# Graph norm of a GNN kernel: variance with features on partitions instead of along the row

## What is computed

```
def _batchnorm(x, g, b):
    mu = jnp.mean(x, axis=0)
    var = jnp.mean((x - mu) ** 2, axis=0)
    return (x - mu) * jax.lax.rsqrt(var + EPS) * g + b
...
return _batchnorm(conv_out + h_attn + h, norm2_g, norm2_b)
...
x = x + _L1_gnn_ref(_layernorm(x, axis=-1), ...)
x = x + _L1_ffn_ref(_layernorm(x, axis=-1)[None], ...)[0]
```

## Time and profile before

| | us |
|---|---|
| median of 3 runs | 1284.91 (1284.19 to 1285.83) |
| profiled execution, own time | 1289.82 |
| its span | 1288.10 |
| granted TensorE clock, mean of the span | 0.983 of full speed |
| TensorE busy | 1219.5 (95%) |
| VectorE busy | 547.9 (43%) |
| ScalarE busy | 452.7 (35%) |
| GpSimd busy | 227.7 (18%) |

### The profile page before, as it was taken

The page is one execution under the profiler, slowest core; times in us unless marked ns, Lnnn a source line. Parts: engine busy times, 40 slices in busy tenths (PEclk is TensorE's granted clock), DMA queues, the critical chain, the costliest instruction groups (busy, mean ns, idle before and its releaser), DMA issues. The chain is left out here.

```text
span 1288.1 us, 19378 instructions
## 1 busy us (share of the span) xinstructions
PE 1219.5 (95%) x6528; PEld 814.0 (63%) x6529; DVE 547.9 (43%) x1535; ACT 452.7 (35%) x965; POOL 227.7 (18%) x227
## 2 busy tenths in 40 slices
PE   4999899999999899999999999999989999989898
PEld 2555476468448555478877887786555587564465
DVE  8999743433443344110000000001296345675784
ACT  6878533233223310011111111111123343338873
POOL 1000070030000008311111111111273000025540
PEclk9999899999999989999999999999998999999899
DMA  9300000000003300671165312564562010100011
GB/s 221 91 1 1 1 2 1 0 2 2 0 6 126 130 2 1 203 273 42 44 245 182 115 44 70 216 236 148 167 186 98 1 35 1 74 0 1 1 31 52
DMA packets 42978, 98.25 MB, mean 76 GB/s; under 512 B 4142, under 2 KB 6632, under 8 KB 41874
## 3 DMA queue, kind: packets, MB, share of 16 engines
q1 hardware_dynamic: 28642, 68.70, 16.0%
q0 software_dynamic: 6144, 16.45, 4.6%
q10 hardware_dynamic: 8112, 12.08, 2.6%
HBM read 81.02 MB, written 16.17 MB: 75 GB/s over the span
## 5 line engine op out<-in xcount | busy, mean ns | idle before, releaser
L498 PEld LDWEIGHTS psum<-sb_blk,sb_w_reg 128*128 128x128 f32 x1792 | 204.0, 192 | 12.8 <-issue 12.8
L498 PE MATMUL psum<-sb_blk,sb_w_reg 128*128 128x128 f32 x1792 | 205.2, 275 | 1.7 <-issue 1.7
L2145 PE MATMUL psum<-sb_z_reg_r,sb_hT_conv_r 125*125 125x512 f32 x385 | 156.9, 408 | 0.4 <-DVE sb_z_last L1262 0.4
L1434 DVE TENSOR_TENSOR sb_blk<-sb_blk,psum 128x256 f32<-128x256 f32 x56 | 23.6, 421 | 277.0 <-ACT sb_blk L955 277.0
L2145 PE MATMUL psum<-sb_htok_r,sb_hT_conv_r 125*125 125x512 f32 x285 | 112.9, 396 | 0.0
L498 PE MATMUL psum<-sb_hT_conv,sb_w_reg 128*128 128x416 f32 (+3 forms) x336 | 103.6, 465 | 0.8 <-ACT sb_hT_conv L532 0.8
L2235 PE MATMUL psum<-sb_w_reg,sb_blk 128*128 128x512 f32 x224 | 100.8, 592 | 0.0
L498 PEld LDWEIGHTS psum<-sb_hT_conv,sb_w_reg 128*128 128x128 f32 x336 | 63.8, 193 | 35.9 <-issue 33.0
L2145 PEld LDWEIGHTS psum<-sb_z_reg_r,sb_hT_conv_r 125*125 125x125 f32 x385 | 72.0, 187 | 18.0 <-issue 0.7
L2067 PE MATMUL psum<-sb_w_reg,sb_hT_conv 128*125 128x512 f32 x160 | 83.1, 613 | 0.0
L955 ACT ACTIVATE sb_blk<-psum 128x256 f32<-128x256 f32 x56 | 21.5, 384 | 162.9 <-PE psum L498 160.1
(11 more groups left out here) (452 smaller groups left out, 2002.3 us busy)
## 6 DMA issues: line engine op xcount, KB each, us to landing
sb_hT_conv<-w_expert SPq DMA_DIRECT2D x7, 2048.0 KB, 9.8
sb_w_reg<-w_expert SPq DMA_DIRECT2D x6, 2048.0 KB, 18.1
sb_hT_conv<-w_expert SPq DMA_DIRECT2D x7, 1024.0 KB, 12.4
slot_outs<-sb_blk ACTq DMA_DIRECT2D x28, 256.0 KB
sb_w_reg<-w_expert SPq DMA_DIRECT2D x6, 1024.0 KB, 19.9
sb_w_reg<-w_gnn SPq DMA_DIRECT2D x1, 4096.0 KB
sb_w_reg<-w_qkv SPq DMA_DIRECT2D x1, 3072.0 KB, 21.5
slot_outs<-sb_blk ACTq DMA_DIRECT2D x1, 2560.0 KB, 13.1
```

The costliest lines, as they stand in the source:

```text
L498: ins = e.matmul(out, l, r, start=(n == 0), stop=(n == len(pairs) - 1))
L1434: e.tensor_tensor(hidT[:, 2 * h:2 * h + 2, :].rearrange("p k n -> p (k n)"), silg[:, h, :], psum[:, 1 + h, HF:2 * HF], ALU.mult).then_inc( ...
L2145: ins = e.matmul(psum[0:TP, b, :], counts_at(l, 2 * i + n // NT)[:, s % HALF_T, :], z[s], start=(n == 0), stop=(n == len(pairs) - 1))
```

## The change

The squares become the stationary operand, in four blocks of 128 features, and the first column of `mean_w` the moving one, so that the variance stands as 128 partitions x 4 columns in bank 1. These columns are set to zero first by a matmul with a zeroed operand, since four accumulations share the bank. The root and the reciprocal are taken of 128x4. VectorE multiplies the identity by each of the four columns, and TensorE multiplies a matrix of ones by the four results, which puts the row of 512 reciprocals into 125 rows of bank 1; VectorE multiplies that by the norm's weights into `sc2`. The four ones matmuls stand behind the first two values products on TensorE, the other six behind them, and three filler matmuls remain of eight. The semaphore `centered` is now called `stat_vec` and counts the four products too.

```diff
--- before.py
+++ after.py
@@ -348,9 +348,12 @@
         rden = s3[:, 228:244].rearrange("p (t h) -> p t h", t=2)
         bst = s3[:, 250:322].rearrange("p (k c s) -> p k c s", k=KD, c=3)
         bmv = s3[:, 322:330].rearrange("p (k s) -> p k s", k=KD)
+        none4 = s3[0:TP, 340:340 + KD]
         bsc, bsh = s3[:, 330:334], s3[:, 334:338]
         squares = a_reg[0:TP, 0:NT * D].rearrange("p (t n) -> p t n", n=D)
         sc2 = w_reg[0:TP, 1, 1552:1552 + D]
+        by_feature = a_reg[:, 0:D].rearrange("p (k c) -> p k c", k=KD)
+        std4 = a_reg[:, D:D + KD]
         scale = DH ** -0.25
         inv_root_m = M_FEAT ** -0.5
 
@@ -468,8 +471,8 @@
         at_turned, attnT_in, ha_mm, ha_in, shifted = (
             sem(n) for n in ("at_turned", "attnT_in", "ha_mm", "ha_in", "shifted"))
 
-        conv_added, y_ready, stat_mm, centered, squared, searched, var_std, scaled_vec, scaled_pool, x_two = (
-            sem(n) for n in ("conv_added", "y_ready", "means_and_variances", "centered", "squared", "rest_searched",
+        conv_added, y_ready, stat_mm, stat_vec, squared, searched, var_std, scaled_vec, scaled_pool, x_two = (
+            sem(n) for n in ("conv_added", "y_ready", "means_and_variances", "stat_vec", "squared", "rest_searched",
                              "var_std", "scaled_vec", "scaled_pool", "x_two"))
 
         ia_mm, ia_in, chosen_pool, proc_mm, acts_in = (
@@ -1180,10 +1183,10 @@
 
             e.wait_ge(neigh_mm, 4 * NT)
             for i in range(NT):
-                e.wait_ge(centered, i + 1)
+                e.wait_ge(stat_vec, i + 1)
                 e.square(squares[:, i, :], htok[:, i, :]).then_inc(squared, 1)
             e.wait_ge(stat_mm, 2)
-            e.activation(sc2, psum[0:TP, 1, :], ACT.Sqrt, bias=eps[0:TP, :]).then_inc(var_std, 1)
+            e.activation(std4, psum[:, 1, 0:KD], ACT.Sqrt, bias=eps).then_inc(var_std, 1)
             for j in range(4):
                 e.wait_ge(pv_mm, j + 1)
                 e.copy(w_po_flat[:, j * 512:(j + 1) * 512], psum[:, 4 + j, :]).then_inc(pv_in, 1)
@@ -1974,6 +1977,7 @@
             for n, i in enumerate(Y_ORDER):
 
                 if n == 2:
+                    e.memset(none4, 0.0).then_inc(v_own, v.up())
                     e.wait_ge(y_ready, 2)
                     e.tensor_tensor(y_sum, htok[:, Y_ORDER[0], :], htok[:, Y_ORDER[1], :], ALU.add).then_inc(v_own, v.up())
                 elif n > 2:
@@ -1989,11 +1993,14 @@
                                 ALU.add).then_inc(y_ready, 1)
             e.wait_ge(stat_mm, 1)
             for i in range(NT):
-                e.tensor_tensor(htok[:, i, :], htok[:, i, :], psum[0:TP, 0, :], ALU.subtract).then_inc(centered, 1)
+                e.tensor_tensor(htok[:, i, :], htok[:, i, :], psum[0:TP, 0, :], ALU.subtract).then_inc(stat_vec, 1)
             e.wait_ge(var_std, 1)
-            e.reciprocal(sc2, sc2).then_inc(v_own, v.up())
-            e.wait_ge(v_own, v.n)
-            e.tensor_tensor(sc2, sc2, rows3[:, 1, :], ALU.mult).then_inc(scaled_vec, 1)
+            e.reciprocal(std4, std4).then_inc(v_own, v.up())
+            e.wait_ge(v_own, v.n)
+            for k in range(KD):
+                e.tensor_scalar(by_feature[:, k, :], ident, std4[:, k:k + 1], None, ALU.mult).then_inc(stat_vec, 1)
+            e.wait_ge(stat_mm, 3)
+            e.tensor_tensor(sc2, psum[0:TP, 1, :], rows3[:, 1, :], ALU.mult).then_inc(scaled_vec, 1)
             e.wait_ge(scaled_vec, 1)
             e.wait_ge(squared, NT)
             for t in range(NT + 3):
@@ -2598,16 +2605,26 @@
                 pe_conv_sum(e, flag, i)
             e.wait_ge(y_ready, NT)
             e.matmul(psum[0:TP, 0, :], mean_w, y_sum, start=True, stop=False)
+            e.matmul(psum[:, 1, 0:KD], ident[0:TP, :], none4, start=True, stop=False)
             e.wait_ge(y_ready, NT + 1)
             e.matmul(psum[0:TP, 0, :], mean_w, htok[:, NT - 1, :], start=False, stop=True).then_inc(stat_mm, 1)
             for i in range(NT):
                 e.wait_ge(squared, i + 1)
-                ins = e.matmul(psum[0:TP, 1, :], mean_w, squares[:, i, :], start=(i == 0), stop=(i == NT - 1))
+                for k in range(KD):
+                    ins = e.matmul(psum[:, 1, k:k + 1], squares[:, i, k * 128:(k + 1) * 128], mean_w[:, 0:1],
+                                   start=False, stop=(i == NT - 1 and k == KD - 1))
             ins.then_inc(stat_mm, 1)
             e.wait_ge(ha_in, 4)
-            for k in range(8):
+            for k in range(2):
                 pe_values(e, k)
-            pe_busy(e, 2, w_o[:, 0, :], 8)
+            for k in range(KD):
+                e.wait_ge(stat_vec, NT + k + 1)
+                ins = e.matmul(psum[0:TP, 1, k * 128:(k + 1) * 128], one16[:, 0:1].to_broadcast([128, TP]),
+                               by_feature[:, k, :], start=True, stop=True)
+            ins.then_inc(stat_mm, 1)
+            for k in range(2, 8):
+                pe_values(e, k)
+            pe_busy(e, 2, w_o[:, 0, :], 3)
 
             for i in range(NT):
                 e.wait_ge(ln_out, 3 * NT + i + 1)
```

## The result

The changed kernel is slower. The first comparison gave a median of 1297.63 us (1292.68 to 1298.51, 4 executions) against 1285.37 (1284.19 to 1286.01, 4): ratio 1.0087, interval 1.0066 to 1.0108, so 8.5 to 13.9 us. It was compared twice more, beside the experiments: 1.0055 (1.0042 to 1.0068) and 1.0049 (1.0034 to 1.0064), so 4.4 to 8.8 us. The forecast was +7.4 us with 1288.4 to 1295.2; the direction came true, the first median lies 2.4 us above the range.

A forecast was written before the change was run, and what follows sets the result against it. Bound: TensorE's squares, a 4.9 us serial chain, then VectorE's tile loop. Squares +6.9, serial part +0.0, ScalarE's queue +1.4, GpSimd -0.95 gave +7.4: 1292.3 us, range 1288.4 to 1295.2.

The forecast's parts named there:

- Squares, +6.9 forecast: TensorE's squares as 80 one-column records, 0.214 us each at 1.2 GHz, end at 1128.9 against 1122.0 us: +6.9.
- I take 1.2 GHz for the whole stretch: Squares: the clock has already fallen when they begin and one-column work does not raise it; 17.1 us for 80 loads.
- a sign against it: Changed profile, squares: a granted clock of 1.00 during them would show the forecast wrong.
- lower bound: Range's low side: a fall 2.6 to 3.5 us after short work begins ends squares up to 3.4 us earlier, 1288.9.
- Serial part, +0.0 forecast: Root to scales: 4.9 us again, the reciprocal's gain taken by half-speed values products and the ones matmuls.
- ScalarE's queue against GpSimd, +1.4 - 0.95 forecast: Before the first turn: VectorE waits 1.4 us for ScalarE's copies and root; GpSimd's earlier end gives back 0.95.
- Filler, 0 forecast, at most +1.5: Ahead of the turns: five removed fillers hide entirely; TensorE idles 2.3 us, up to +1.5 if the clock falls.
- The clock coming back on continuously issued loads: Rival at the squares: weight loads keep TensorE busy, full clock from 1114.7; 1284.2 us, same; chance 0.12.
- The rival of a full clock throughout: Rival at the squares: no fall ahead of them and the clock holds, 8.6 us of loads; 1282.4 us; chance 0.02.
- The half case: Squares: full clock for part of the stretch, 3 to 4 us less, about 1288.6 us; chance 0.10.
- first rival: Squares: the clock comes back all the same at 1114.7; 1284.2 us, no change that can be told; chance 0.12.
- I carry the difference over to the median: Whole kernel: the profiled execution, 4.91 us above the median, gives the change in time, +7.4, added to 1284.9.

The follow-up runs named there:

- wide: Changed kernel with all 125 columns of mean_w moving in the squares' matmuls in place of one; 1285.35 us against 1287.28 for the kernel before, ratio 0.9986.
- after_again: The changed kernel as it is, compared and traced once more; 1293.02 us against 1287.28 for the kernel before, ratio 1.0055.
- late_copies: Changed kernel with ScalarE's last two copies of the values product moved behind the roots of tiles 0 and 1; 1293.70 us against 1287.28, ratio 1.0049.
- fill8: Changed kernel with eight filler matmuls ahead of the turns again in place of three; 1295.30 us against 1287.28 for the kernel before, ratio 1.0067.
- dense_turns: 125-column squares, five fillers ahead of the turns, one after the first turn, two after the second; 1287.73 us against 1292.00 before, ratio 0.9977.
- before_gap: Kernel before the change with values products 0 and 1 moved between the mean and the squares; 1292.17 us against 1292.00, ratio 1.0001.
- best: 125-column squares, values 0 and 1 before them, value 2 before the ones matmuls, one late copy, fillers between turns; 1287.70 us against 1292.00 before, ratio 0.9976.
- after: The changed kernel in its first comparison and trace; 1297.63 us against 1285.37 for the kernel before, ratio 1.0087.
- after_third: The changed kernel as it is, a third time; 1300.24 us against 1293.19 for the kernel before, ratio 1.0049.
- before: The kernel without the change, in its only trace; median 1285.37 us in the first comparison.
- cover1: 125-column squares, one values product ahead of the ones matmuls, ScalarE's last copy behind tile 0's root; 1289.62 us against 1292.00 before, ratio 0.9993.

## Why the prediction was right in direction and wrong in number

**Squares, +6.9 forecast.** The mechanism held: 80 records, 0.213 us apart at 1.2 GHz, and in none of the five traces with one-column squares did the clock hold or come back in them. In wide the same number of records and loads, with 125 columns, took 10.7 us. The size was 5.1 to 5.4 in four of the five traces with one-column squares and 6.9 in after_again. This term was mis-sized, in the step "I take 1.2 GHz for the whole stretch": in four of them the clock was at 1.00 when the squares began, which the prediction had named as a sign against it, and fell 1.7 to 2.0 us after the first square. The forecast had a later fall only in its lower bound. (By the window of the earlier trace rows the fall behind L2194 is at 169.2 and not 169.4, so 3.3 us after the short work began and not 3.5.)

**Serial part, +0.0 forecast.** +0.1 to +0.5 in the four traces in which the clock fell during the squares, +1.2 where the ones matmuls too ran at half clock. Reciprocal 0.18 (0.17 said), root 0.26 (0.30), four products 0.87 (1.0), ones 1.04 (0.9). At full clock (wide) the part is 3.4 us, so the serial part gains 1.5 us there, and half-speed values products ate that gain in the changed kernel, as argued.

**ScalarE's queue against GpSimd, +1.4 - 0.95 forecast.** VectorE waited 1.22 at L519 and the first L524 took 0.53 in place of 1.49; to the first turn it was 9.1 us against 8.8, +0.3 where +0.5 was forecast. late_copies takes the wait away and gets 0.27 us between GpSimd's start and the first turn.

**Filler, 0 forecast, at most +1.5.** This step failed: "they hide entirely". TensorE idled ahead of the first turn; in all three traces of the changed kernel the clock fell behind the turns, and turn to activation took 23.5 to 24.4 us in place of 22.6: +0.8 to +1.8. I had priced this fall and put it among the bounds, although the change's own gap of 2.3 us (2.15 measured) spoke for it. That the missing fillers are the whole reason is not shown: fill8, with all eight back, still had a fall, of half the length. dense_turns, with five ahead of the first turn and three between the turns, had none there.

**The sum.** +5.4 + 0.15 + 0.3 + 1.7 = +7.5 in the first pair of traces, forecast +7.4: two errors of about 1.6 us against each other, so the agreement is partly luck.

**The rivals.** The clock coming back on continuously issued loads didn't happen in any of five traces; once down, the grant stayed at 0.50 to the end of the squares, for 13.4 us and more with TensorE busy. By the Trainium skill (TensorE: Matmul & The Clock Gate, Part 1) activity releases the throttle. These five traces don't agree, for TensorE was busy to the end of the squares and the full clock didn't return; the squares of wide, where it came back 3.1 us after the first, do. The rival of a full clock throughout didn't come either (the prediction's 1282.4 for it should be 1282.6, 1.6 below the first rival's 1284.2). The half case deserved more than 0.10: in four of five traces the squares lie between it and the forecast.

**The number.** The first median lies 2.4 us above the range. The step that failed for the number is "I carry the difference over to the median", with a range made of this stage's bounds alone: the stage measured +7.5, +9.5 and +7.6 us, the medians +12.3. The profiled execution before was 4.9 us above its median, which showed that executions differ by more than this stage does, and I gave it no width. With the two later ratios, 1284.91 x 1.0055 and x 1.0049 are 1292.0 and 1291.2, beside the forecast's 1292.3. Why the first comparison, with four executions on each side, gave 4 to 5 us more stays open: its interval overlaps that of the second only just and not that of the third, and only the fastest of its four changed executions has a trace. From the first square to the end of the span it is 184.6 to 185.8 us in the three traces of the changed kernel and 176.5 before, so 8.1 to 9.3 us more and not 12. By an estimate from these and the spans on record, the three slower changed executions (1295.0 to 1296.0) reached the first square at 1109 to 1111 us, the profiled one at 1106.34: the missing microseconds would lie ahead of the stage, where squares started anywhere from 1104.2 to 1114.6 in the twelve traces. Whether the two waits shown above made the difference in those executions, no trace of them tells.

## What to carry to other kernels

Price a reduction that is turned into one-column matmuls by its weight loads, and at the lower of TensorE's clocks too: here 80 records cost 17.3 us at 1.2 GHz, 8.6 at 2.4 (an estimate from 0.107 us each), and giving the same loads 125 columns to move won 6.6 us. Before taking filler or dense work out, look at where TensorE waits next: before_gap had no fall at one gap and had it at the following one, and only best, with work in both, ran the whole stage at full clock, in both its traces. Where executions spread by several microseconds in a stage that the change doesn't touch, compare start times within the changed stage, and widen the range for the whole by that spread.

## What the runs showed of the hardware that was not expected

A TensorE that the profile shows busy can still lose its clock: L2614 in the changed kernel was issued without a gap for 15.7 us, with a 128-column load at every record, and the clock went from 1.00 to 0.50 in it. With 125 moving columns the interval at full clock is 0.114 us (80 records in 9.13 us in best), against 0.107 for the two columns of L2546.

The clock at which squares begin differs from one execution to the next, with the same code ahead of them but for the zeroing: 1.00 in the traces of after, fill8, late_copies and after_third, 0.50 in those of before, after_again and wide (down 0.3 to 0.7 us before the first square), 1.00 and held in that of cover1, and in that of dense_turns it fell 0.1 us after the first square. What decides between them is open. And TensorE's turns with gaps of 1.3 to 2 us between them held the full clock in before and lost it in eight other traces. In seven of these TensorE waited 1.3 to 2.2 us ahead of the first turn, where before it had worked up to it; fill8, which had no such wait, lost it latest and for 3.4 us only.
